# A two-layer transformer kernel on one core: its opening, its routing, one row-turn order and the way the last rows are stored

## What is computed

```python
x = x + _L0_xattn_ref(_layernorm(x), ctx, ...)   # banded attention (|i-j| <= 64), 8 heads of 16, over 512 positions
x = x + _L0_ffn_ref(_layernorm(x), w1, w2, w3)    # SwiGLU, 512 -> 1408 -> 512, weights rounded to NF4 and back
x = x + _L1_xattn_ref(_layernorm(x), ctx, ...)   # cross attention, 16 heads, int8-rounded projections
x = x + _L1_ffn_ref(_layernorm(x), ...)           # mixture of 32 experts, top 6, plus a shared expert
```

```python
scores = jnp.sqrt(jax.nn.softplus(logits))
_, topk_idx = jax.lax.top_k(scores + bias[None, :], K)      # K = 6 of E = 32
topk_w = jnp.take_along_axis(scores, topk_idx, axis=1)
topk_w = topk_w / jnp.sum(topk_w, axis=-1, keepdims=True) * SCALE
pos = jnp.cumsum(onehot, axis=0) - 1                         # place of a row in its expert's list, CAP = 192
routed = (yb[eid, pos] * w_slot[:, None]).reshape(-1, K, Hd).sum(axis=1)
```

## Time and profile before

| | us |
|---|---|
| median of 3 runs (lowest, highest) | 1501.9 (1497.35, 1503.89) |
| the profiled execution | 1502.36 |
| its span, first to last instruction | 1500.6 |

### The profile page before, as it was taken

How to read it: one execution, slowest core, us unless ns; L and a number is a source line. 1 busy time by engine, 2 the same in 40 slices (tenths; PEclk the granted TensorE clock), 3 DMA queues, 4 the chain that set the end, 5 groups by cost and what they waited for, 6 DMA issues and landing times. The chain is left out here.

```text
span 1500.6 us, 28677 instructions
## 1 busy us (share of the span) xinstructions
PE 1359.7 (91%) x8666; PEld 816.4 (54%) x8666; DVE 1013.0 (68%) x3256; ACT 786.9 (52%) x1796; POOL 224.8 (15%) x263
## 2 busy tenths in 40 slices
PE   3678999999999899999989999997698999999994
PEld 1344555555555444444455556664344777777872
DVE  6889999999997545546456788777498555554101
ACT  4777888888878533332267666766420233333320
POOL 2100000000000000000021000000011355555543
PEclk7699999999999999999999999999798999999998
DMA  8434343443420300000010000000612588888973
GB/s 263 127 88 102 87 113 99 98 107 91 121 79 10 127 0 0 0 0 1 0 43 15 15 15 14 14 2 1 237 60 102 173 255 252 256 253 252 258 180 49
DMA packets 62647, 148.53 MB, mean 99 GB/s; under 512 B 10730, under 2 KB 27800, under 8 KB 58350
## 3 DMA queue, kind: packets, MB, share of 16 engines
q1 hardware_dynamic: 48718, 113.64, 24.9%
q0 software_dynamic: 13856, 33.98, 9.9%
HBM read 112.16 MB, written 35.39 MB: 98 GB/s over the span
## 5 line engine op out<-in xcount | busy, mean ns | idle before, releaser
L778 DVE CUSTOM_DVE_ANT_0 masked_scores<-ps_max,band_mask 128x192 bf16<-128x192 f32 (+1 forms) x512 | 177.5, 384 | 19.0 <-PE ps_max L506 12.3
L386 ACT ACTIVATE probs_t<-ps_sc 128x448 f32<-128x448 f32 x256 | 138.7, 542 | 80.7 <-PE ps_sc L526 78.2
L1220 PE MATMUL f_ps<-f_xt,w_t 128*128 (+1 forms) x704 | 160.2, 382 | 5.9 <-ACT w_t L1257 2.6
L380 ACT ACTIVATE nf_above<-nf_scaled,nf_sign_at 128x512 f16<-128x512 bf16 x231 | 161.6, 715 | 0.0
L2691 DVE TENSOR_TENSOR d_inter<-d_silu_g,d_su 128x384 f32<-128x384 f32 x32 | 17.7, 554 | 160.0 <-PE d_su L2396 154.8
L1811 ACT ACTIVATE c_probs<-c_s,c_negmax 128x128 f32<-128x128 f32 x256 | 90.3, 364 | 64.5 <-DVE c_negmax L1896 64.1
L506 PE MATMUL ps_max<-k_stack,q_stack 96*128 96x192 bf16 (+1 forms) x512 | 96.3, 272 | 28.5 <-DVE row_max L778 18.0
L1220 PEld LDWEIGHTS f_ps<-f_xt,w_t 128*128 128x128 bf16 x704 | 69.2, 98 | 89.7 <-issue 7.7
L2255 POOL DMA_INDIRECT out<-d_h,d_scatter_now x64 | 96.9, 1514 | 102.0 <-DMA out<-d_h,d_scatter_now 82.8
L2565 DVE TENSOR_SCALAR d_onehot<-d_slot_no,d_pos 128x192 bf16<-128x192 bf16 x512 | 101.8, 289 | 0.3 <-PE d_lb L2319 0.3
L506 PEld LDWEIGHTS ps_max<-k_stack,q_stack 96*128 96x128 bf16 x512 | 46.2, 101 | 101.0 <-issue 51.6
(11 more groups left out here) (341 smaller groups left out, 2761.5 us busy)
## 6 DMA issues: line engine op xcount, KB each, us to landing
d_wgu<-in_ex_gu SPq DMA_DIRECT2D x32, 1024.0 KB, 5.9
d_wdown<-in_ex_d SPq DMA_DIRECT2D x32, 512.0 KB, 5.9
dr_parts<-qk_parts SPq DMA_DIRECT2D x32, 384.0 KB, 4.8
q_stack<-dr_parts SPq DMA_DIRECT2D x32, 192.0 KB, 2.7
k_stack<-dr_parts SPq DMA_DIRECT2D x32, 192.0 KB, 3.4
out<-x_sb SPq DMA_DIRECT2D x17, 256.0 KB, 2.1
nf_w<-in_nf_w POOLq DMA_DIRECT2D x3, 1408.0 KB, 9.1
q_stack<-dr_parts SPq DMA_DIRECT2D x32, 128.0 KB, 2.4
```

Source lines behind the costliest of these rows:

```text
L380: act.activation(above[:, g, k, :], lvl[:, g, :], ACT.Sign, bias=cut[:, k - NDV:k - NDV + 1]).then_inc(s_sg, 1)
L386: act.activation(pt[:, c, :], SP[c % 2][:].rearrange("p a w -> p (a w)")[:, a:z], ACT.Exp, scale=D0 ** -0.5).then_inc(s_e, 1)
L778: op = dve.tensor_tensor_reduce(masked[:, c % 2, k, off:off + hi - lo], M[c % 2][:, k, off:off + hi - lo], mask[:, k, off:off + hi - lo], ...
L1220: mm = pe.matmul(bank[:], w12[:, m, kt, ft * P:(ft + 1) * P], xt[:, q, kt, bass.ds(g * N, N)], start=(kt == 0 and q == 0), stop=(kt == KT ...
```

## The change

- The ones of `k_stack` are written by a GpSimd memset of the two partitions (2 x 8192 bf16) after its input loads; `k_ones`, DVE's memset and SyncE's DMA go.
- ACT makes the row sums of rows 4 to 7 before the parts of batch 1. DVE's residuals and third parts of batch 1 move behind the reduction L886.
- In the feed-forward, row tiles 2 and 3 are turned before the last `down`.
- In the routing, the top 6 of each row are replaced in a copy of the selection values (`match_replace`), and the mask is where copy and original differ. The values get two more columns, preset so that the unused two of the eight places match there.
- The gathers of the first four experts wait for three of five list steps and read the indices in place.
- At the end SyncE reads the last group's rows of `out` back into `x_sb` once all scatters have landed; DVE adds the shared expert's part to them, and SyncE stores them. PE writes the four tiles to four banks without waiting for the additions.

```diff
@@ opening: sync, gpsimd
-            sp.wait_ge(s_k1, 1)
-            sp.dma_start(kst[96:98].rearrange("p b h t -> p (b h) t"),
-                         k_ones[:].rearrange("p (o t) -> p o t", o=1).broadcast_to((2, 2 * H0, D))).then_inc(s_ko, 16)
...
             load_nf(0)
             for k in range(2, len(X_AT) - 1):
                 load_x(pool, k)
+            pool.wait_ge(s_cx, 7)
+            pool.memset(kst[96:98], 1.0).then_inc(s_ko, 1)
             pool.wait_ge(s_am, 1)
             gather_maxima(0, 1)
@@ opening: scalar
             root(2, DVE_ROWS)
+            for b in range(DVE_ROWS, DVE_ROWS + 4):
+                row_sum(b)
             for k in range(2):
                 first_part(1, 1, k)
             for k in range(2):
                 second_part(1, k)
-            for b in range(DVE_ROWS, NB):
+            for b in range(DVE_ROWS + 4, NB):
                 row_sum(b)
@@ opening: vector
-            dve.memset(k_ones[:], 1.0).then_inc(s_k1, 1)
...
             v_copy(0, 0)
-            resid_part(1, 0)
-            resid_part(1, 1)
-            third_part(1, 0)
-            third_part(1, 1)
...
             dve.wait_ge(s_wn[0], 16)
             dve.tensor_reduce(sc1[:, 0:MNB], blocked(wn[:, 0:MCOL]), AX.X, ALU.max, apply_absolute_value=True).then_inc(s_am, 1)
+            resid_part(1, 0)
+            resid_part(1, 1)
+            third_part(1, 0)
+            third_part(1, 1)
             for c in range(8):
                 take_max(0, 0, c)
@@ feed-forward: tensor
                     turn_rows(XBANK[1], g + 1, 1)
-                down(n, g, LAST, LAST % 2)
-                if not last:
                     pe.wait_ge(s_h, n + FREE + 1)
                     turn_rows(XBANK[2], g + 1, 2)
                     turn_rows(XBANK[3], g + 1, 3)
+                down(n, g, LAST, LAST % 2)
@@ mixture: gather
-                pool.wait_ge(s_lst, 5 * q + 5)
-                if not isinstance(e, int) or e >= 4:
+                here = isinstance(e, int) and e < 4
+                pool.wait_ge(s_lst, 5 * q + (3 if here else 5))
+                if here:
+                    at, at_pair = gidx[:, e:e + 1], gpair[:, e // 2:e // 2 + 1]
+                else:
+                    at, at_pair = gst[:, buf, 0:1], gsp[:, buf // 2, 0:1]
                     pool.wait_ge(s_xt, e - 3)
...
@@ mixture: end, gpsimd and sync
             scatter(NE - 1, 1, False)
-            pool.wait_ge(s_kv, 5)
-            pool.wait_ge(s_sc, 32 * NE)
-            for c in range(4):
-                pool.wait_ge(s_add, 4 * NS + c + 1)
-                pool.nop(nofuse=True)
-                pool.indirect_dma_start(out, bass.IndirectOffsetOnAxis(ap=fidx[:, c:c + 1], axis=0),
-                                        x[:, 4 * NS + c, :], None, compute_op=ALU.add).then_inc(s_sh, 16)
-            pool.wait_ge(s_sh, 64)
...
             quads(sp, body)
+            sp.wait_ge(s_sc, 32 * NE)
+            for c in range(4):
+                sp.dma_start(x[:, 4 * NS + c], outr[:, 4 * NS + c]).then_inc(s_bk, 16)
+            for c in range(4):
+                sp.wait_ge(s_add, 4 * NS + c + 1)
+                sp.dma_start(outr[:, 4 * NS + c], x[:, 4 * NS + c]).then_inc(s_sh, 16)
+            sp.wait_ge(s_sh, 64)
@@ mixture: tensor, vector
-                    ge(pe, s_add, 4 * j + c - 1)
+                    if j < NS:
+                        ge(pe, s_add, 4 * j + c - 1)
...
-            def last_rows(b):
+            def last_rows(c):
+                b = 4 * NS + c
                 dve.wait_ge(s_y, b + 1)
-                dve.tensor_copy(x[:, b, :], YB[b % 2][:]).then_inc(s_add, 1)
+                dve.wait_ge(s_bk, 64)
+                dve.tensor_tensor(x[:, b, :], x[:, b, :], LAST[c][:], ALU.add).then_inc(s_add, 1)
@@ mixture: routing on vector
             for b in range(NB):
-                op = dve.max(top[:, b, :], val[:, b, :])
+                op = dve.max(top[:, b, :], val[:, b, 0:NE])
             chain(op)
+            chain(dve.memset(top[:, :, TOPK:8], UNUSED))
+            dve.wait_ge(s_k, 7)
             for b in range(NB):
-                op = dve.max_index(topi[:, b, :], top[:, b, :], val[:, b, :])
+                op = dve.match_replace(left[:, b, :], top[:, b, :], val[:, b, :], TAKEN)
             chain(op)
-            chain(dve.tensor_copy(topf[:], topi[:]))
             gated(0)
-            dve.wait_ge(s_k, 7)
-            iob = ioe[:].rearrange("p (o e) -> p o e", o=1).broadcast_to((P, NB, NE))
-            for k in range(TOPK):
-                dst = mask if k == 0 else a
-                chain(dve.tensor_tensor(dst[:], iob, topf[:, :, k:k + 1].broadcast_to((P, NB, NE)), ALU.is_equal))
-                if k:
-                    chain(dve.tensor_tensor(mask[:], mask[:], a[:], ALU.add))
-            chain(dve.tensor_copy(maskb[:], mask[:]))
+            chain(dve.tensor_tensor(maskb[:], left[:, :, 0:NE], em[:], ALU.not_equal))
```

More of the change, by code:

```diff
@@ L2176, in phase_layer1_moe @@
     SOFTPLUS = 11
-    MASKED = SOFTPLUS + 4 + 2 * TOPK
+    MASKED = SOFTPLUS + 5
+    TAKEN, UNUSED = -3.0e38, -3.2e38
     LISTED = MASKED + 11
@@ L2199, in _ @@
         def _(pool):
-            pool.iota(ioe[:], [[1, NE]], base=0, channel_multiplier=0, allow_small_or_imprecise_dtypes=True).then_inc(s_k, 1)
+            pool.memset(val[:, :, NE:], UNUSED).then_inc(s_k, 1)
             pool.iota(iof[:], [[1, CAP]], base=0, channel_multiplier=0, allow_small_or_imprecise_dtypes=True).then_inc(s_k, 1)
@@ L2225, in gather @@
             def gather(e, buf, q):
[L2227 to L2234 removed]
+                here = isinstance(e, int) and e < 4
[4 more added lines that the diff above has]
+                    at, at_pair = gst[:, buf, 0:1], gsp[:, buf // 2, 0:1]
+                    pool.wait_ge(s_xt, e - 3)
+                    pool.tensor_copy(gst[:, buf, :], gidx[:, bass.ds(e, 1)]).then_inc(s_gi, 1)
+                    if buf % 2 == 0:
+                        pair = 2 * q + buf // 2
+                        pool.tensor_copy(gsp[:, buf // 2, :], gpair[:, bass.ds(pair, 1)]).then_inc(s_gpi, 1)
+                    pool.wait_ge(s_gi, e - 3)
                 pool.wait_ge(s_hw, 16 * NG)
@@ L2237, in gather @@
                 pool.indirect_dma_start(xg[:, buf, :], None, h_dram,
-                                        bass.IndirectOffsetOnAxis(ap=gst[:, buf, 0:1], axis=0)).then_inc(s_gt[buf], 16)
+                                        bass.IndirectOffsetOnAxis(ap=at, axis=0)).then_inc(s_gt[buf], 16)
                 if buf % 2 == 0:
-                    pool.wait_ge(s_gpi, pair + 1)
+                    if not here:
+                        pool.wait_ge(s_gpi, pair - 1)
                     pool.nop(nofuse=True)
                     pool.indirect_dma_start(xgp[:, buf // 2, :], None, h_dram,
-                                            bass.IndirectOffsetOnAxis(ap=gsp[:, buf // 2, 0:1], axis=0)).then_inc(s_gp[buf // 2], 16)
+                                            bass.IndirectOffsetOnAxis(ap=at_pair, axis=0)).then_inc(s_gp[buf // 2], 16)
             def scatter(e, par, start):
@@ L2349, in shared_down @@
                 for c in tiles:
-                    ge(pe, s_add, 4 * j + c - 1)
+                    if j < NS:
+                        ge(pe, s_add, 4 * j + c - 1)
                     for it in range(IT):
-                        mm = pe.matmul(YB[c % 2][:], si[:, j % 2, it, c * P:(c + 1) * P], sd[:, it, :], start=(it == 0), stop=(it == IT - 1))
+                        mm = pe.matmul((YB[c % 2] if j < NS else LAST[c])[:], si[:, j % 2, it, c * P:(c + 1) * P], sd[:, it, :], start=(it == 0), stop=(it == IT - 1))
                     mm.then_inc(s_y, 1)
@@ L2599, in _ @@
             dve.wait_ge(s_act, 1)
-            e_ = b_
+            e_, em = b_, val[:, :, 0:NE]
             chain(dve.tensor_scalar(a[:], e_[:], 1.0, None, ALU.add))
-            chain(dve.tensor_scalar(val[:], a[:], -1.0, None, ALU.add))
-            chain(dve.tensor_scalar(pos[:], val[:], 0.0, None, ALU.is_equal))
-            chain(dve.tensor_scalar(val[:], val[:], 2.0 ** -24, None, ALU.max))
-            chain(dve.reciprocal(mask[:], val[:]))
+            chain(dve.tensor_scalar(em[:], a[:], -1.0, None, ALU.add))
+            chain(dve.tensor_scalar(pos[:], em[:], 0.0, None, ALU.is_equal))
+            chain(dve.tensor_scalar(em[:], em[:], 2.0 ** -24, None, ALU.max))
+            chain(dve.reciprocal(mask[:], em[:]))
             dve.wait_ge(s_act, 2)
             chain(dve.tensor_tensor(c_[:], c_[:], mask[:], ALU.mult))
-            chain(dve.scalar_tensor_tensor(out=c_[:], in0=val[:], scalar=2.0 ** -24, in1=c_[:], op0=ALU.is_gt, op1=ALU.mult))
+            chain(dve.scalar_tensor_tensor(out=c_[:], in0=em[:], scalar=2.0 ** -24, in1=c_[:], op0=ALU.is_gt, op1=ALU.mult))
             chain(dve.tensor_tensor(c_[:], c_[:], pos[:], ALU.add))
@@ L2647, in _ @@
             chain(dve.tensor_tensor(vals[:, :, :, 4], sc[:], vals[:, :, :, 3], ALU.subtract))
```

(2 more changed lines are left out.)

33 lines of the change are left out of this document (10 added, 23 removed).

## The result

| | before | after |
|---|---|---|
| median of the runs (lowest, highest), us | 1502.9 (1497.4, 1505.0), 4 runs | 1482.4 (1476.1, 1485.6), 4 runs |
| ratio, 95% interval | | 0.9864 (0.9821 to 0.9908) |
| the profiled execution / its span | 1502.4 / 1500.6 | 1476.1 / 1474.4 |

A forecast was written before the change was run, and what follows sets the result against it. PE, busy 91% of the span, was taken as the bound, so only its waits and the kernel's start and end pay. Terms 2.6 + 2.2 + 0.5 + 1.4 + 1.3 + 3.4 = 11.4 us; 1501.9 - 11.4 = 1490.5 us, range 1485.5 to 1497.

The forecast's parts named there:

- Opening: Kernel start: earlier reduction brings the first maximum forward, though GpSimd's memset holds DVE's cast; 2.6 us won.
- Its end of -4.1: Opening's best case: DVE isn't held by the memset, so 4.1 us are won.
- rival (c): Opening: DVE isn't held by the memset; 1.5 us more won, 1489.0 us; chance 0.1.
- Turns: Feed-forward's three group boundaries: turning tiles 2 and 3 before the last `down` wins 0.75 us each, 2.2 us.
- Routing: Mask for the experts: shorter DVE work, nearly all beside PE, so only 0.5 us won.
- Gathers: Before the first expert: first gather issued 1.4 us earlier, and the pair's rows arrive 1.3 us faster.
- Rival (a): First expert: shorter stop keeps TensorE's clock up; 3.3 us more won, 1487.2 us; chance 0.2.
- End: Kernel end: reads, DVE additions and plain stores replace four accumulating DMAs; last landing 1487.8 instead of 1491.2, 3.4 us won.
- Rival (b): Opening wins nothing: parts land as late as before, +1.5 instead of -2.6, 1494.6 us; chance 0.15.
- (d): End: reads take 8 us, winning about 1 us; with half the opening's failure, 1495 to 1496; chance 0.15.
- (e): Opening: slow memset (32 us) holds DVE throughout, opening ends 22 us later, kernel 1515 us; chance 0.05.

The follow-up runs named there:

- o1: Kernel after, but the ones written as in before (DVE memset and SyncE DMA), no GpSimd memset: 1481.8 us, one run.
- o3: Kernel after, with GpSimd's memset of the ones held until the third parts of batch 0 are written: 1483.0 us, one run.
- o4: o1 with one more wait, so GpSimd writes the block maxima only after PE's first score products: 1484.0 us, ratio 0.988.
- the new end alone: Kernel before with only the new end (four banks, read back, stores): 1490.2 us against 1500.7, ratio 0.9932.
- the wait on SyncE: Kernel before, with SyncE instead of GpSimd waiting for the four last accumulating DMAs to land: ratio 0.998.
- the shifted code: Kernel before with 64 empty instructions more in GpSimd's list, early in the mixture: 1498.2 us, one run.
- the turns alone: Kernel before with only the feed-forward change, all four row tiles turned ahead of the last `down`: 1505.5 us, one run.
- k2: Kernel after with three unused 128x512 products on PE in the stop before the first expert: 1478.3 us, ratio 0.9831.

## Why the prediction was off

The terms of the sum, against what the traces and runs give for each:

- **Opening**, -2.6: 3.0 (3.4 between the middle values of five and six profiles). The chain of the forecast held link by link. Its end of -4.1, and with it rival (c), fell: without the hold the first maximum is later (o1 to o3) or the same (o4), not 1.5 us earlier. I had left PE at 28.86 in that case, though the early reduction sends a DMA in front of the stack loads. I had given this write 0.3 us.
- **Turns**, -2.2: 1.9. The new wait for `f_hparts` was named; it is 0.54 us at each boundary.
- **Routing**, -0.5: 0.6, and the mask is ready first.
- **Gathers**, -1.4 and -1.3: 2.7 together in the two profiles, but only the first term was the change's. The first gather goes out 1.35 us earlier in every profile. For the second I took the 6.4 us of the earlier trace rows as the price of the old gathers. From the issue of the pair's gather to PE's turn it is 6.5 us in that profile of before, and 5.3 to 5.4 in the four others with the old gathers (the new end alone, the wait on SyncE, the shifted code, the turns alone); with the new gathers it is 4.8 to 5.2 in ten. The stop itself is 4.5 to 4.6 us in these four. So this term is worth 0.1 to 0.6 us and not 1.3, both terms about 1.7, and that the pair of profiles agreed with 2.7 was luck. Rival (a) didn't happen: a stop of 2.97 us brings the clock down as well as one of 5.66. In the profiles with this stop unfilled `up` takes 4.2 to 5.5 us. Its price was right all the same, since k2 wins 2.9 us with a stop of 0.25 us.
- **End**, -3.4: 4.0 for what I had priced. The step of the prediction that failed is the clause behind it: "behind this come 9.4 us in which nothing runs, which I leave as they are". I took the tail as a constant of the kernel. It was GpSimd's closing, 6.3 us of it a DRAIN and 2.9 a gap ahead of it, and the change takes GpSimd out of the last place: 0.4 us are left of the 9.4. The row was in the trace of before; the views that I had read, the timeline and the chain of the engines' work, leave it out, and the question to ask of an idle tail is which engine's queue fills it.

By the two profiles the priced terms come to 3.0 + 1.9 + 0.6 + 2.7 + 4.0 = 12.2 us, where 11.4 were forecast; with 1.7 for the gathers it is 11.2. The tail adds 9.0: 20.2 to 21.2, against 20.4 and 21.6 by the two comparisons. The profiles differ by 5 us more since that of before has three dips of the clock that this one of after lacks; the stretches in which they lie hold 2.0 + 1.7 + 1.1 = 4.8 us.

Rival (b), the opening wins nothing, failed as the parts landed in 4.4 to 5.2 us; (d) as the reads landed when forecast; (e) as the memset took 6.92 us. No rival said that a cost outside the changed steps could go. The lower end of the range has a slip: (a) with (c) is 1490.5 - 3.3 - 1.5 = 1485.7, not 1485.5; it decides nothing.

## What to carry to other kernels

An idle tail is work of some queue: look at the source line where the stage ends, and let the last landing be waited for by an engine that has nothing slow to close. GpSimd's closing can run beside the last DMAs of another queue, and it is worth keeping it off the last place even if nothing else changes (3 us for one moved wait here). Before removing a stall at a crowded time, write down which transfers it keeps in order: in this opening three ways of removing or moving it made the first maximum later, and a fourth won nothing. And a price read from one landing in one profile can be that execution's own: the pair's gather took 6.5 us in one and 5.4 in four others.

## What the runs showed of the hardware

- GpSimd's DRAIN at the end of the last stage took 5.9 to 6.3 us when it began behind the landing of its last DMA, even over 10 us behind. When it began before the landing, it ended 4.6 to 4.8 us behind it (eleven profiles). SyncE's took 0.007 to 0.12 us.
- A GpSimd memset of a contiguous stretch is paid per element of a partition: 8192 in 6.92 us, as 2x8192 bf16 or 128x8192 f32, and the same bytes as 2x4096 f32 in 3.51.
- With one write of 22 KB from 21.2 us on, the queues carried 68 GB/s between 22 and 26 us instead of 157, and the median landing of the stack loads was 1.8 us later.
- TensorE's clock fell to its lower level after stops of 1.8 to 3.0 us in some executions and not in others (2.61 us before the same 32 products: 7.08 or 8.76 us). A fill by products without use kept it up each of the three times.
